# A four-layer graph network on one core: row statistics made in the stages ahead, and a fourth ScalarE evaluation per group in the second nucleus step

## The chip, the cores and the metric

The kernel runs on one core of a Trainium2 chip. The metric is the device time of one execution in microseconds (us), as the median over several runs. The core has five engines that work side by side and meet at semaphores: TensorE (PE in the profile, its weight loads PEld), VectorE (DVE), ScalarE (ACT), GpSimd (POOL) and SyncE (SP), which here only issues DMAs.

## The reference, cut to what matters

x is 2048 x 256, adj is 2048 x 2048. Each of four layers takes the row-normalised x, cuts it at zero and adds its result to x.

```python
h = relu(_layernorm(x)); x = x + L0(h)     # 8-head attention with adj as bias and mask
h = relu(_layernorm(x)); x = x + L1(h)     # two diffusion steps, then a layernorm with gamma and beta
h = relu(_layernorm(x)); x = x + L2(h)     # normalised adj @ h @ W.T + b
h = relu(_layernorm(x)); x = x + L3(h)     # relu(normalised (adj + I) @ h @ weight)

# L1, for each of two steps s:
Xf = Rf @ Xf;  Xb = Rb @ Xb
Xa = A @ Xa            # A = _adj_from_feats(Xa): softmax of the logits over the "nucleus" of each row
Z  = Z + (Xf @ U1[s] + Xb @ U2[s] + Xa @ U3[s])
# at the end: Y = X + Z, then (Y - mean) / sqrt(var + eps) * gamma + beta
```

The nucleus of a row holds its largest softmax weights until their sum reaches 0.9; the rest of the row is dropped and the row is normalised again.

## The kernel before, in words

The 2048 rows are held as T = 16 row blocks of 128 partitions. The program is a sequence of stages, each a block with one instruction stream per engine, with a barrier between blocks: setup, adjacency, `attend` (L0), then for step 0 and step 1 of L1 a `refresh` (called qk0 and qk1, which makes the logit factors) and a `nucleus` (nuc0 and nuc1), then `onward` (the end of L1 and the start of L2) and `last` (L2 and L3). Nothing plans the order at run time: on each engine it is the order in which the Python functions issue the instructions, and the semaphore waits between them decide the rest.

**attend.** For each of 8 heads and 16 row blocks TensorE makes logits (`qk`, L638), VectorE adds the bias and finds the row maximum (`peaks`, L786), ScalarE takes exp and rounds to fp16 (L706, L711), VectorE makes the fp16 remainder (`lo`, L800), SP turns both halves by DMA, and TensorE multiplies (`av`, L649). `add` (L811) adds to acc and `shift` (L870), in the last head, stores x with beta added to x_scratch. GpSimd makes two powers and one `partition_all_reduce` (L699) near the start and is then idle.

**refresh, with norm (qk0).** VectorE takes `bn_stats` and `bn_aggr` of acc in quads of four row blocks and adds eps; GpSimd takes the power -1/2 (L1370); VectorE makes the bias (`centre`, L1499); ScalarE writes the normalised rows (L1437); TensorE transposes them (L1386), and multiplies. TensorE also waits for `halved`, the halving of w3 (L1504) after its load.

**nucleus.** Rows are worked on in four groups of G = 4 row blocks. For each row block i = G*g + k TensorE makes the logits (L1687), VectorE finds the peak (L2024), ScalarE takes exp into e (L1882, `exp(g, k)`). Then a threshold per row is searched by C = 7 evaluations (step 1): an evaluation sums the weights of a row over a threshold, and `update` narrows the bounds. It is done in one of two ways:

- `cut(g, n)` on VectorE: four `mass` instructions (L2027), one per row block, and `update`.
- `sums(g, n)` on ScalarE: two instructions per row block, Relu and Sign with accumulation (L1896), which write their full output into PT (`aside`), and on VectorE `update_from_sums(g, n)`. VectorE asks for it with `aim(g)`; `next_sums(g, n)` is `update_from_sums` and `aim`. The constant BY_SUMS = 3 says how many of the seven are of this kind in groups 1 to 3 of step 1.

After the seven, `look(g)` settles the threshold, and `keep(g, n)` removes what is under it, with the ties, tile by tile (L2202, L2212). Each finished tile is multiplied: TensorE turns it (`multiply(g, k)`, L1702), ScalarE copies it in eight pieces into the two fp16 tiles PT (`halves(g, k)`, L1904 and L1906), and TensorE multiplies with the rows of x (L1720). The logits of group g + 1 share one PSUM buffer, so `logits(g + 1, k + 1)` waits for `exp(g + 1, k)`.

Beside that runs the diffusion of Xf and Xb (`diffuse`, L1620 to L1665) with ScalarE's part in `results`: `rows_of` (L1849), `turned_rows` (L1858, L1860) and `weighted_rows` (L1864, which writes y). In step 1 the row blocks 0 to 4 are diffused beside group 0 and 1, 5 to 8 after `multiply(0, 3)`, 9 to 12 after `multiply(1, 3)`, 13 to 15 after `multiply(2, 3)` (DIFFUSED = (5, 9, 13)). After each of the last three stands a row of `after(n)` (L1754 to L1760, L1917, L1919), which adds the last product of row block n to y. ScalarE's order in step 1, around the change:

```python
sums(1, 2)
for k in range(G):
    halves(0, k)
    exp(2, k)
    product(0, k)
for n in range(BY_SUMS):
    sums(2, n)
    results(range(DIFFUSED[0] + n, DIFFUSED[0] + n + 1), n > 0)
```

The last group is turned by `last_halves` (L1933) and `last_rests` (L2305, VectorE).

**onward.** For each quad of row blocks: statistics of y, a power on GpSimd (L985), y centred and multiplied by gamma (`centre`, L1077), added onto x (`onto`, L1085), statistics of x, a power, the bias (`aim`, L1092), the normalised rows on ScalarE (`normal`, L1030), transposes and the product with W on TensorE (L998, L1007), two cuts on ScalarE (L1045, L1048) and the remainder on VectorE (L1098). SP loads w2, W3, the row b, then x in four pieces, and when all have landed the 16 pieces of adjT, which `last` reads.

## Time and profile before

| what | value |
|---|---|
| median of 3 runs | 3354.73 us (3354.25 to 3355.26) |
| profiled execution | 3354.33 us, its span 3352.5 us |
| busy share of the span | PE 88%, PEld 66%, DVE 65%, ACT 40%, POOL 2% |
| mean granted TensorE clock | 0.953 |

The stages in the span: attend about 190 to 1890 us, qk0 to 1939, nuc0 to 2396, qk1 to 2412, nuc1 to 3100, onward to 3159, last to the end. The times below are microseconds from the start of the span. A row of a timeline gives the start, the duration, the engine, the line of the kernel, the operation and its operands, how many instructions are merged in it, and in brackets how long the engine had been idle before it and what released it. The line of an instruction is the one in the printed kernel. Buffer numbers are left out of names: nuc_e is e, nuc_l the PSUM banks, nuc_pThi and nuc_pTlo are PT, nuc_minus_t the negated threshold.

### The profile page before, as it was taken

The numbers are of one execution on the slowest core, as the hardware profiler recorded it, in microseconds if no ns is written. First come the engines' busy times: TensorE is split into PE (matmuls) and PEld (weight loads), VectorE is DVE, ScalarE is ACT, GpSimd is POOL, SyncE is SP. The second block draws the span as 40 slices with busy tenths as digits, with TensorE's granted clock in tenths as the row PEclk, the third lists the DMA queues.
The fourth block names the chain that finished last, engine by engine and source line by source line (L and its number), as shares of the span: only waits on it lengthen the run. The fifth ranks groups of instructions, "written<-read, shape, count | busy, mean of one in ns | idle before, by whom it ended". The sixth has DMA issues, their size and how long they took to land. (4 is left out here: it accounts for less than half of the span.)

```text
span 3352.5 us, 56595 instructions
## 1 busy us (share of the span) xinstructions
PE 2954.3 (88%) x20632; PEld 2221.0 (66%) x20632; DVE 2162.5 (65%) x4428; ACT 1349.0 (40%) x1750; POOL 57.8 (2%) x71
## 2 busy tenths in 40 slices
PE   3989999999999999999999778878884678687699
PEld 3966776767767677676776447656563556575588
DVE  7865655556555565555656488888588887885531
ACT  5844434444344443444434322333326355522321
POOL 0000000000000000000000000000000000000100
PEclk8999999999999999999999889999997889899899
DMA  7938748477484774847748412100010010100500
GB/s 265 410 133 200 183 119 199 114 190 186 118 199 114 189 186 118 200 114 190 185 119 213 100 57 89 39 5 23 26 39 26 1 51 11 41 26 1 232 1 26
DMA packets 587858, 396.82 MB, mean 118 GB/s; under 512 B 538563, under 2 KB 553414, under 8 KB 562118
## 3 DMA queue, kind: packets, MB, share of 16 engines
q1 hardware_dynamic: 585990, 382.49, 42.3%
q10 hardware_dynamic: 1728, 12.58, 1.1%
q8 instruction: 73, 1.20, 0.1%
q14 instruction: 67, 0.55, 0.0%
HBM read 223.05 MB, written 37.75 MB: 78 GB/s over the span
## 5 line engine op out<-in xcount | busy, mean ns | idle before, releaser
L800 DVE SCALAR_TENSOR_TENSOR e_lo<-e,e_hi 128x2048 f16<-128x2048 f32 x128 | 293.3, 2292 | 432.2 <-ACT e_hi L711 432.2
L649 PE MATMUL av<-vw_hi,pT_hi 128*128 128x256 f16 x2048 | 559.7, 273 | 6.2 <-DMA pT_lo<-e_lo 6.2
L649 PE MATMUL av<-vw_lo,pT_hi 128*128 128x256 f16 x2048 | 559.7, 273 | 0.0
L649 PE MATMUL av<-vw_hi,pT_lo 128*128 128x256 f16 x2048 | 559.7, 273 | 0.0
L638 PE MATMUL logits<-kT_hi,qT_hi 128*128 128x512 f16 x1024 | 389.6, 380 | 4.6 <-DVE att_small L786 4.0
L638 PE MATMUL logits<-kT_lo,qT_hi 128*128 128x512 f16 x1024 | 389.1, 380 | 0.0
L638 PE MATMUL logits<-kT_hi,qT_lo 128*128 128x512 f16 x1024 | 389.1, 380 | 0.0
L705 ACT ACTIVATE att_small<-att_small,minus 128x1 f32<-128x1 f32 x128 | 38.0, 297 | 772.9 <-DVE att_small L795 772.9
L786 DVE CUSTOM_DVE_ANT_0 e<-logits,bias,att_small 128x1024 f32<-128x1024 f32 x256 | 328.6, 1283 | 0.0
L2027 DVE SCALAR_TENSOR_TENSOR nuc_junk<-nuc_e,nuc_thr 128x2048 bf16<-128x2048 f32 x140 | 323.7, 2348 | 3.9
L706 ACT ACTIVATE e<-e,att_small,sc 128x2048 f32<-128x2048 f32 x128 | 266.5, 2082 | 0.0
L711 ACT ACTIVATE e_hi<-e 128x2048 f16<-128x2048 f32 x128 | 244.7, 1912 | 15.3
L649 PEld LDWEIGHTS av<-vw_hi,pT_hi 128*128 128x128 f16 x2048 | 200.9, 98 | 43.2 <-issue 6.7
L649 PEld LDWEIGHTS av<-vw_lo,pT_hi 128*128 128x128 f16 x2048 | 200.9, 98 | 36.3
L649 PEld LDWEIGHTS av<-vw_hi,pT_lo 128*128 128x128 f16 x2048 | 200.9, 98 | 23.8
L1687 PE MATMUL nuc_l<-logit_k,logit_q 128*128 128x512 f32 x256 | 133.9, 674 | 65.9 <-ACT nuc_e L1882 58.9
L638 PEld LDWEIGHTS logits<-kT_hi,qT_hi 128*128 (+1 forms) x1024 | 100.3, 98 | 123.1 <-issue 15.4
L638 PEld LDWEIGHTS logits<-kT_hi,qT_lo 128*128 (+1 forms) x1024 | 100.4, 98 | 121.6 <-issue 1.3
L638 PEld LDWEIGHTS logits<-kT_lo,qT_hi 128*128 (+1 forms) x1024 | 100.5, 98 | 107.2 <-issue 1.1
L1663 PE MATMUL nuc_l<-nuc_u,nuc_xsT 128*128 128x256 f32 x320 | 92.0, 444 | 77.2 <-ACT nuc_xsT L1860 68.6
L382 PE MATMUL adj_tp<-ident_one,adj_rows 128*128 128x129 f32 x512 | 123.1, 404 | 30.5 <-DVE adj_count L418 30.5
L382 PEld LDWEIGHTS adj_tp<-ident_one,adj_rows 128*128 128x128 f32 x512 | 123.0, 337 | 30.8 <-DVE adj_count L418 30.8
(427 smaller groups left out, 5777.0 us busy)
## 6 DMA issues: line engine op xcount, KB each, us to landing
bias<-bias_scratch SPq DMA_DIRECT2D x130, 1024.0 KB, 4.9
bias_scratch<-adj_bias SPq DMA_DIRECT2D x16, 1024.0 KB, 8.3
adjT_scratch<-adjT SPq DMA_DIRECT2D x16, 1024.0 KB, 8.5
nuc_at_hi<-adjT_scratch SPq DMA_DIRECT2D x32, 512.0 KB, 3.8
nuc_at_lo<-adjT_scratch SPq DMA_DIRECT2D x32, 512.0 KB, 4.6
adjT<-adjT_scratch SPq DMA_DIRECT2D x16, 1024.0 KB, 19.9
adj_rows<-in_adj_dram ACTq DMA_DIRECT2D x12, 1024.0 KB, 8.7
adj_rows<-in_adj_dram SPq DMA_DIRECT2D x4, 1024.0 KB, 14.0
```

Source lines behind the costliest of these rows:

```text
L382: last = nc.tensor.matmul(o, rows_u[:, t // 2, t % 2 * P:(t % 2 + 1) * P], ident1[:, :], start=True, stop=True)
L638: last = nc.tensor.matmul(o, QT[w][:, k, ds(t * P, P)], KT[x][:, k, c0:c0 + BANK], start=(k == 0 and w == x == 0), stop=(k == 1 and w == 1))
L649: last = nc.tensor.matmul(AV[par], PT[par][w][:, m, :], VW[x][:, m, :], start=(m == 0 and w == x == 0), stop=(m == T - 1 and w == 1))
L705: nc.scalar.activation(masked(par), nb(par), ACT.Exp, bias=minus[:, 0:1], scale=1.0)
L706: nc.scalar.activation(E[par][:, :], E[par][:, :], ACT.Exp, bias=nb(par), scale=sc[:, 0:1], accum_out=ssum(par)).then_inc(exped, 1)
L711: nc.scalar.activation(EH[:, :], E[par][:, :], ACT.Copy, scale=P_SCALE).then_inc(hi_s, 1)
L786: return nc.vector.tensor_tensor_reduce(E[par][:, cols], L[half][:, :], B[par][:, cols], 1.0, (small[:, par, 6:7], m0(par))[half], ALU.add ...
L800: nc.vector.scalar_tensor_tensor(out=EL[:, :], in0=E[par][:, :], scalar=P_SCALE, in1=EH[:, :], op0=ALU.mult, op1=ALU.subtract).then_inc(lo ...
L1663: nc.tensor.matmul(WEIGHTED, xT[:, n * D + k * P:n * D + (k + 1) * P], U[:, n, k, :], start=(n == k == 0), stop=False)
L1687: last = nc.tensor.matmul(scores_in(i)[:, b * BANK:(b + 1) * BANK], QT[:, i * P:(i + 1) * P], KT[:, b * BANK:(b + 1) * BANK], start=True, ...
L2027: nc.vector.scalar_tensor_tensor(out=void[:, k % 2, :], in0=e[:, g % 2, k, 0:N], scalar=bound[:, k:k + 1], in1=e[:, g % 2, k, 0:N], op0=co ...
```

## The change

1. **Sums.** BY_SUMS becomes 4 for step 1. In groups 1 to 3 evaluation 3 goes from VectorE (`cut(g, 3)`) to ScalarE (`sums(g, 3)`). It is asked for by `next_sums(g, 2)`, which `keep` of the group before now issues ahead of its fourth tile (`behind`), and read by `update_from_sums(g, 3)`. For groups 1 and 2 that stands behind the first peak of the next group. In ScalarE's program sums(1, 3) stands right behind sums(1, 2) and ahead of halves(0, 0); sums(2, 3) and sums(3, 3) stand ahead of the results of row blocks 8 and 12.
2. **Statistics of x for L1.** `attend` makes them in the last head, tile by tile, into `row_stats` (in the place of deg); qk0 only adds eps, takes the powers and makes the bias. A fourth power in attend's GpSimd program follows the all-reduce.
3. **Statistics of y.** At the end of nuc1, VectorE makes them for row blocks 0 to 11 and centres these; GpSimd takes their power. `onward` does it for the last quad only. Its order on VectorE is shorter, and SP loads the first piece of x ahead of w2 and b, and W3 last.
4. **Order.** In attend, ahead of the loop, peaks(1, 1) goes before lo(0, 0). The last head's items are written out instead of looped.

```diff
-        BY_SUMS = (1, 3)[step]
+        BY_SUMS = (1, 4)[step]
...
                 if step:
                     sums(1, 2)
+                    sums(1, 3)
...
                 for n in range((9, 4)[step]):
                     spread(n + 1)
+                if step:
+                    pl.wait_ge(tail_asked, 1)
+                    nc.gpsimd.tensor_tensor(y_rstd[:, 0:DONE], y_rstd[:, 0:DONE], halfp[:, 0:DONE], ALU.pow).then_inc(tail_powed, 1)
...
-                def keep(g, n):
+                def keep(g, n, behind={}):
...
                     for k in range(G):
+                        if k in behind:
+                            behind[k]()
                         load(G + k)
                         first_of_ties(g, k).then_inc(masked_s, 1)
...
-                    keep(0, 1)
-                    update_from_sums(1, 2)
+                    keep(0, 1, {3: lambda: next_sums(1, 2)})
                     peak(2, 0)
-                    cut(1, 3)
+                    update_from_sums(1, 3)
                     peak(2, 1)
...
-                    keep(1, 2)
-                    update_from_sums(2, 2)
+                    keep(1, 2, {3: lambda: next_sums(2, 2)})
                     peak(3, 0)
-                    cut(2, 3)
+                    update_from_sums(2, 3)
...
-                    keep(2, 3)
-                    update_from_sums(3, 2)
-                    for n in range(3, C):
+                    keep(2, 3, {3: lambda: next_sums(3, 2)})
+                    update_from_sums(3, 3)
+                    for n in range(4, C):
                         cut(3, n)
...
                 for k in range(G):
                     last_rests(k)
+                if step:
+                    v.wait_ge(c_done, DONE)
+                    for t in range(DONE):
+                        nc.vector.bn_stats(y_stats[:, t, :], y[:, t, :]).then_inc(tail_s, 1)
+                    v.wait_ge(tail_s, DONE)
+                    for t in range(DONE):
+                        nc.vector.bn_aggr(row_stats[:, t, :], y_stats[:, t, :]).then_inc(tail_s, 1)
+                    v.wait_ge(tail_s, 2 * DONE)
+                    nc.vector.tensor_scalar(y_rstd[:, 0:DONE], row_stats[:, 0:DONE, 1], LN_EPS, None, ALU.add).then_inc(tail_asked, 1)
+                    for t in range(DONE):
+                        nc.vector.scalar_tensor_tensor(out=y[:, t, :], in0=y[:, t, :], scalar=row_stats[:, t, 0:1], in1=gb[:, 0, :],
+                                                       op0=ALU.subtract, op1=ALU.mult).then_inc(tail_s, 1)
+                    v.wait_ge(tail_s, 3 * DONE)
```

In attend:

```diff
                 pl.wait_ge(ratios, 1)
                 nc.gpsimd.partition_all_reduce(top[:, 4:7], top[:, 0:3], P, ABSMAX).then_inc(largest, 1)
+                pl.wait_ge(largest, 1)
+                nc.gpsimd.tensor_tensor(top[:, 7:8], scales[:, 2, 0:1], halfp[:, 0:1], ALU.pow).then_inc(largest, 1)
...
+                def statistics(t):
+                    v.wait_ge(av_free, T * (HEADS - 1) + t + 1 + AV_FREE)
+                    nc.vector.bn_stats(summary, acc[:, t, :]).then_inc(summed_up, 1)
+                    v.wait_ge(summed_up, 2 * t + 1)
+                    nc.vector.bn_aggr(row_stats[:, t, :], summary).then_inc(summed_up, 1)
+                    v.wait_ge(summed_up, 2 * t + 2)
...
                 evacuate(0, 3)
+                link.wait()
+                peaks(1, 1, 1, link)
                 lo(0, 0, link)
-                peaks(1, 1, 1, link)
```

In refresh and onward:

```diff
-                    stats_of(0)
-                    v.wait_ge(w_loaded, 16 * 5)
-                    nc.vector.tensor_scalar(w3[:, :, :, :], w3[:, :, :, :], 0.5, None, ALU.mult).then_inc(halved, 1)
-                    for b in range(1, QUADS):
-                        stats_of(b)
-                        centre(b - 1)
+                    for b in range(QUADS):
+                        q = slice(QUAD * b, QUAD * (b + 1))
+                        nc.vector.tensor_scalar(rstd[:, q], mv[:, q, 1], LN_EPS, None, ALU.add).then_inc(stats_done, 1)
+                    for b in range(QUADS - 1):
+                        centre(b)
+                        if b == 1:
+                            v.wait_ge(w_loaded, 16 * 5)
+                            nc.vector.tensor_scalar(w3[:, :, :, :], w3[:, :, :, :], 0.5, None, ALU.mult).then_inc(halved, 1)
                     centre(QUADS - 1)
...
-                stats_of(0, 0)
-                stats_of(0, 1)
-                centre(0)
+                stats_of(0, 3)
                 row_scales()
                 onto(0)
                 stats_of(1, 0)
                 weights_in()
-                stats_of(0, 2)
+                onto(1)
                 aim(0)
-                centre(1)
-                onto(1)
                 stats_of(1, 1)
-                stats_of(0, 3)
+                centre(3)
+                onto(2)
                 aim(1)
-                centre(2)
-                onto(2)
                 stats_of(1, 2)
-                centre(3)
+                remainder(0)
                 aim(2)
-                remainder(0)
                 onto(3)
                 stats_of(1, 3)
                 remainder(1)
```

## Rows read from the trace of the kernel before

**Rows 1.** Windows: length; busy PE, PEld, DVE, ACT, POOL; PEclk, DMA share, GB/s

```profile
2412.00:3100.00 688.00, 507.10 (x3440) 399.87 (x3440) 547.08 (x1164) 293.04 (x416) 2.30 (x8) 0.89 0.08 27
2758.00:2776.00 18.00, 13.06 (x56) 9.19 (x57) 8.75 (x29) 4.41 (x12) 0.00 (x0) 1.00 0.02 8
```

**Rows 2.** Timeline of ACT, groups 1 to 2 (start us, us; released by)

```profile
2571.50 2.00 ACT L1896 ACTIVATE nuc_pThi<-nuc_e,nuc_minus_t 128x2048 f16<-128x2048 f32 x1 [5.84 <-DVEq L2019]
...
2590.24 0.60 ACT L1904 ACTIVATE nuc_pThi<-nuc_l 128x512 f16<-128x512 f32 x1 [2.73 <-PE nuc_l L1702]
...
2599.05 0.60 ACT L1906 ACTIVATE nuc_pTlo<-nuc_l 128x512 f16<-128x512 f32 x1 [0.48 <-PE nuc_l L1713]
...
2640.03 1.96 ACT L1882 ACTIVATE nuc_e<-nuc_l,nuc_nmax 128x2048 f32<-128x2048 f32 x1
...
2670.29 1.96 ACT L1882 ACTIVATE nuc_e<-nuc_l,nuc_nmax 128x2048 f32<-128x2048 f32 x1
```

**Rows 3.** Timeline of DVE, groups 1 to 2

```profile
2535.68 0.17 DVE L2061 SCALAR_TENSOR_TENSOR nuc_signs<-nuc_signs,nuc_half_t 128x4 f32<-128x4 f32 x1 [0.33 <-ACT nuc_pTlo L1896]
...
2538.95 2.35 DVE L2145 SCALAR_TENSOR_TENSOR nuc_junk<-nuc_e,nuc_hi 128x2048 f32<-128x2048 f32 x1
...
2607.99 0.09 DVE L2202 MATCH_VALUE_LOAD nuc_junk<-nuc_listed,nuc_e 128x8 f32 x1 [0.21 <-issue]
...
2620.02 2.29 DVE L2024 TENSOR_REDUCE nuc_nmax<-nuc_l 128x1 f32<-128x2048 f32 x1
...
2672.38 0.17 DVE L2040 TENSOR_SCALAR nuc_work<-nuc_Z 128x4 f32<-128x4 f32 x1 [3.40 <-ACT nuc_e L1882]
```

**Rows 4.** Timeline of ACT, groups 2 to 3

```profile
2736.67 0.60 ACT L1858 ACTIVATE nuc_xsT<-nuc_l 128x512 f32<-128x512 f32 x1
...
2743.20 0.39 ACT L1864 ACTIVATE y<-nuc_l 128x256 f32<-128x256 f32 x1 [4.92 <-PE nuc_l L1665]
...
2757.79 0.39 ACT L1864 ACTIVATE y<-nuc_l 128x256 f32<-128x256 f32 x1 [2.18 <-PE nuc_l L1665]
```

**Rows 5.** Timeline of DVE, groups 2 to 3

```profile
2756.55 0.09 DVE L2202 MATCH_VALUE_LOAD nuc_junk<-nuc_listed,nuc_e 128x8 f32 x1 [0.22 <-issue]
...
2778.24 2.29 DVE L2024 TENSOR_REDUCE nuc_nmax<-nuc_l 128x1 f32<-128x2048 f32 x1 [9.61 <-PE nuc_l L1687]
```

**Rows 6.** Timeline of ACT, group 3 and the tail

```profile
2921.36 0.39 ACT L1864 ACTIVATE y<-nuc_l 128x256 f32<-128x256 f32 x1 [2.18 <-PE nuc_l L1665]
...
2939.57 0.60 ACT L1904 ACTIVATE nuc_pThi<-nuc_l 128x512 f16<-128x512 f32 x1 [0.82 <-PE nuc_l L1702]
...
3045.45 2.07 ACT L1933 ACTIVATE nuc_pThi<-nuc_l 128x512 f16<-128x512 f32 x4
```

**Rows 7.** Timeline of DVE, group 3 and the tail

```profile
2920.18 0.09 DVE L2202 MATCH_VALUE_LOAD nuc_junk<-nuc_listed,nuc_e 128x8 f32 x1 [0.22 <-issue]
...
3059.12 2.47 DVE L2305 SCALAR_TENSOR_TENSOR nuc_pTlo<-nuc_l,nuc_pThi 128x512 f16<-128x512 f32 x4
```

**Rows 8.** Costliest groups, second nucleus step, shapes apart

```profile
L2027 DVE SCALAR_TENSOR_TENSOR nuc_junk<-nuc_e,nuc_thr 128x2048 bf16<-128x2048 f32 x76 | 175.7, 2348 | 2.2
```

**Rows 9.** Timeline of PE, start of attention and of qk0

```profile
251.96 0.60 PE L638 MATMUL logits<-kT_hi,qT_hi 128*128 128x512 f16 x1 [3.97 <-DVE att_small L786]
...
1903.98 0.87 PE L1386 MATMUL qk_tp<-ident,y 128*128 128x128 f32 x3 [14.74 <-ACT y L1437]
```

**Rows 10.** Timeline of POOL, first power of qk0

```profile
1900.46 2.05 POOL L1370 TENSOR_TENSOR qk_rstd<-qk_rstd,halfp 128x4 f32<-128x4 f32 x2 [1670.75 <-DVE qk_rstd L1494]
```

**Rows 11.** Timeline of DVE, qk0 and onward

```profile
1897.49 0.29 DVE L1504 TENSOR_SCALAR w<-w 128x256 f32<-128x256 f32 x1 [2.30 <-DMA w<-in_L_gnn_W_dram]
...
3102.46 1.40 DVE L1067 BATCH_NORM_STATS2 onw_stats<-y 128x6 f32<-128x256 f32 x4
...
3104.39 1.67 DVE L1077 SCALAR_TENSOR_TENSOR y<-y,onw_mv,gamma_beta 128x256 f32<-128x256 f32 x4
...
3115.86 0.15 DVE L1092 SCALAR_TENSOR_TENSOR onw_minus<-onw_mv,onw_rstd 128x4 f32<-128x4 f32 x1
```

More of the change, by code:

```diff
@@ L884, in _, with item, last_items, items @@
                 LINKS = 6
-                def items(h, ends=False):
+                def item(h, t, par, link):
+                    i = T * h + t
+                    lo(i + 1, 1 - par, link)
+                    peaks(i + 2, t + 2, par, link)
+                    add(i, t, par, link)
+                    masks(t + 3, 1 - par, link)
+                def last_items():
+                    link = Chain(v, chain, 10 + (HEADS - 1) * (LINKS * T))
+                    for t in range(T - 2):
+                        item(HEADS - 1, t, t % 2, link)
+                        shift(T * (HEADS - 1) + t, t, t % 2)
+                        statistics(t)
+                    return link
+                def items(h):
                     with v.Fori(0, T // 2 - 1) as j:
@@ L1350, in refresh @@
         with block:
-            if norm:
+            if norm is not None:
                 @block.sync
@@ L1433, in _ @@
                 for b in range(QUADS + 2):
-                    if norm and b < QUADS:
+                    if norm is not None and b < QUADS:
                         s.wait_ge(centred, b + 1)
@@ L1482, in cut @@
                             link.note(nc.vector.tensor_scalar(parts[1][:, t, :], rest[:, t, :], lo_gain, None, ALU.mult))
[L1484 to L1494 removed]
+                if norm is not None:
                     def centre(b):
@@ L1519, in _, with nucleus @@
                         nc.vector.tensor_copy(QT[:, b * BANK:(b + 1) * BANK], TP[b // 2][b % 2][:, :]).then_inc(w2_read, 1)
-def nucleus(nc, sb, ps, sem, name, QT, KT, parts, out, ident, diffusion, next_logits):
+def nucleus(nc, sb, ps, sem, name, QT, KT, parts, out, ident, diffusion, next_logits, tail):
     weights, at_d, scales, ident16, y, sc, Xp, Xf, Xb, step = diffusion
@@ L1541, in nucleus @@
     w2x, w3x = w2[:, :, :].rearrange("p a n -> p (a n)"), w3[:, :, :, :].rearrange("p k a n -> p k (a n)")
+    (tail_s, tail_asked, tail_powed) = (sem(f"{name}_tail_{s}") for s in ("stats", "asked", "powed"))
+    gb, halfp, row_stats, y_rstd = tail
+    DONE = T - G
     C = CUTS[step]
```

91 lines of the change are left out of this document (43 added, 48 removed).

## The prediction, made before the changed kernel was timed

> **What bounds the kernel now.** I read the windows by stage first, then for each place that the diff touches the timeline of each engine, and looked in it for the wait that ends last. The stage that changes most is the second nucleus step, 2412 to 3100 us, where VectorE is busy 547.08 of 688 us, TensorE 507.10 and ScalarE only 293.04 [rows 1]. The reader is to see that the half-idle ScalarE is no spare engine here: its rows stand in the order in which its program is written, and TensorE waits for it tile by tile.
>
> Between group 1 and group 2 ScalarE's row of sums(1, 2) starts at 2571.50; eight such rows of 2.0 us make 16.0. After them it copies the turned halves of tile 0, from 2590.24 to 2599.65, and then waits until VectorE has found peak(2, 0), which starts at 2620.02 and takes 2.29 [rows 2, 3]. From there the tiles follow each other by a loop through ScalarE and TensorE: exp(2, 1) at 2640.03 and exp(2, 3) at 2670.29, which is 15.13 us a tile, with no wait for VectorE ahead of either. It is VectorE that waits 3.40 us at 2672.38 for the last exp, before it can begin group 2 [rows 3]. So the loop and VectorE are about level, and the loop is slightly the longer.
>
> Between groups 2 and 3 it is plainer: VectorE waits 9.61 us for the logits of peak(3, 0), until 2778.24 [rows 5]. What it waits for is a queue of small steps that all begin after sums(2, 2): turned rows 2736.67, y 2743.20, y again 2757.79, then the last row block, four after(n) and the logits [rows 4]. Here ScalarE and TensorE already set the end.
>
> **The sums: what the edit takes away.** One evaluation a group is four rows of 2.35 us on VectorE [rows 8], 9.4 us, three times. Its update stays.
>
> **What it adds, group 1 to 2.** sums(1, 3) is asked for by the next_sums that now stands ahead of the fourth tile of keep(0, 1). That tile's first instruction stood at 2607.99; a next_sums costs 2538.95 - 2535.68 = 3.3 us [rows 3]; so ScalarE starts at 2611.3 and ends at 2627.3. In ScalarE's program these sums stand ahead of halves(0, 0), which before ran at 2590 under keep, at no cost. Now they run behind: 9.4 us to 2636.7, then exp(2, 0), which before started at 2622.3 behind the peak. Three times 15.13 later exp(2, 3) starts at 2682.1 against 2670.29: **11.8 us later**. I take the steady 15.13 for all three, since TensorE has just worked on halves(0, 0); the first interval of before, 2622.3 to 2640.03, was 17.7 us, which would make it 14.4. The 9.4 us that VectorE no longer works turn into waits: for sums(1, 3), for the logits ahead of each peak, and ahead of begin(2).
>
> **Group 2 to 3.** The fourth tile of keep(1, 2) stood at 2756.55 [rows 5]. Sums(2, 3) then runs from 2759.85 to 2775.85, both in the frame of before. ScalarE may not turn rows(7) ahead of it, as it did at 2749 under keep; that comes now after 2775.85. What follows is known piece by piece: turned rows, weighing at a TensorE that has just idled, y: 2736.67 to 2743.59, 6.9 us; then from the end of the y at 2757.79 (2758.18) through the last row block, four after(n) and logits(3, 0) to 2778.24, 20.1 us [rows 4, 5]. Between them before lay the matmuls of tile 8, which this time TensorE does while ScalarE sums. 2775.85 + 6.9 + 20.1 = 2802.8 against 2778.24: **24.6 us later**. The loop behind it was free of VectorE before and is unchanged.
>
> **Group 3.** Fourth tile of keep(2, 3) at 2920.18 [rows 7], sums(3, 3) to 2939.5, then 6.9 for y and 17.8 (2921.75 to 2939.57) to halves(2, 0): 2964.2 against 2939.57 [rows 6]. From there to last_halves(0) nothing of VectorE's is waited for, so last_halves(0) comes 24.6 later than 3045.45, at 3070.1. Before, 13 us of cover lay there: last_rests(0) started only at 3059.12, when VectorE had finished keep(3, 4) [rows 7]. VectorE gains little: from the start of the fourth tile it had 12.0 us for the tile and update_from_sums (2607.99 to 2620.02 [rows 3]) and 9.4 + 2.4 for an evaluation with its update, 23.8 to the end of cut(3, 3); now 3.3 + 16.0 + 3.1 = 22.4, since it waits for the sums. So the tail starts at 3070.1 + 0.6 instead of 3059.12: **11.6 us later**.
>
> Together 11.8 + 24.6 + 11.6 = +48.0 us.
>
> **The statistics.** At the front of attention peaks(1, 1) now goes ahead of lo(0, 0) on VectorE. TensorE waited 3.97 us for those reads at 251.96 [rows 9] and ran the next matmuls slowly after it. They can start with no wait, but then av(0) waits for the turned lo half, which leaves VectorE 1.9 us later; I take -2.5 us, bounds 0 and -4.0. The added bn_stats and bn_aggr per tile of the last head (about 0.7 us) lie in VectorE's waits for ScalarE and cost nothing; the last one lies under the store of x. If that cover were gone, 0.7.
>
> In qk0 the whole of TensorE waits 14.74 us, until 1903.98 [rows 9]. GpSimd's first power there starts at 1900.46 [rows 10], 5.3 us after it was asked for, although GpSimd had been idle since the all-reduce, 1670.75 us before; the edit puts a power behind that all-reduce, early in attention, and drops the statistics. Then ready comes near 1896.7 and the next condition is late: w3 halved at 1897.49 + 0.29 [rows 11]. Gain 1903.98 - 1897.9 = 6.1; bounds 2.3 (if the late start stays, only the statistics go) and 6.1. I take -6.0: the later powers of that stage start at once after their request.
>
> At the end of step 1 the statistics and centrings of twelve row blocks, three quads at 1.9 us (3102.46 to 3104.39) and 1.67 [rows 11], 10.7 us, follow last_rests(3) and end about 2 us ahead of TensorE's after(15). The power behind them pays the late start (5.3) and 1 to 3 us, and so ends about 1 us beyond the stage: +1.
>
> In onward the first aim stood at 3115.86, 15.3 us after the stage began. Ahead of it now: one quad of y statistics 1.9, the row scales about 1, two additions at 1.7 (as the centring), one quad of x statistics 1.9, the weights about 1, some 1.5 for x to land, since its load is now first on SP's queue ahead of both weights: 10.7 us. The chain behind it (ScalarE, TensorE, ScalarE) keeps its length, with aim(2) 0.6 us late behind remainder(0). Gain 4.5 less 0.5: -4, bounds -1 and -6. The adjT loads start behind the x loads as before and have some 6 us of slack at the end, of which 4 are used.
>
> **Sum.** 48.0 - 2.5 - 6.0 + 1.0 - 4.0 = +36.5. The profiled execution took 3354.33 (span 3352.5), 0.4 below the median of 3354.73, so the sum gives 3390.8 and 3391.2; I write 3391. From no change this kernel's runs can tell about 0.2%, 7 us.
>
> **Rivals.** (1) VectorE keeps setting the end, and ScalarE's queue is harmless. Then groups 1 and 2, where a peak of 2.3 hides more of the wait, save 23.8 + 2.3 - 22.4 = 3.7 each and group 3 1.4, the statistics 11.5: 3354.7 - 20.3 = 3334, faster. VectorE's high busy share speaks for it; the waits of 3.40 and 9.61 us against [rows 3, 5]. It decides if halves(0, 0) or turned rows(7) could run before the added sums, that is if exp(2, 0) could still start by about 2622. Chance 0.06.
> (2) Only the tail differs: the 13 us of cover turn out to hold all of group 3's delay, for example since results 13 to 15 close up. -11.6: 3379. Chance 0.08.
> (3) TensorE's clock stays at its low level, 1.2 GHz, through the thin chains. In 2758 to 2776 TensorE was busy 13.06 us at a granted clock of 1.00 (2.4 GHz), right after dense matmuls [rows 1]. After the added sums it comes from 20 us of idleness into the same thin work; at the low level these 13 us would double, in groups 2 and 3: +26, 3417. Chance 0.08. The Trainium skill, TensorE: Matmul & The Clock Gate, section A second HAM failure mode: psum-queue depth-cycling, says that an array with small idle gaps between its groups of matmuls can swing between the two levels; by that rule the time would go there, and the row at 1.00 in the same thin work speaks against it.
> (4) The fourth evaluation by sums is rounder than the exact one and some tile needs a retry, a bisection with a look: three to five rows of 2.35 us and small ones, 15 to 30 us a tile, 3406 to 3421. Against it: the 76 evaluations of before are just those of the plan, 7 x 4 for group 0 and 3 x 4 x 4 for the others [rows 8]; none is a retry's. Chance 0.03.
> My own case: 0.75.
>
> **Range.** My case alone 3380 to 3402 (the cold first interval +2.6, statistics +7 and -5, group 2 and 3 chains each 2 either way). 3377 to 3404 takes in (2) and leaves out (1), (3) and (4). Faster 0.06, same 0.02, slower 0.92.
>
> **What would show it.** In the second nucleus step the evaluation rows fall from 76 to 64. exp(2, 0) starts 9 to 10 us after the end of sums(1, 3); VectorE's wait at peak(3, 0) grows from 9.6 to over 25 us; last_rests(0) waits for ScalarE's copy; the stage is 734 to 738 us long. In qk0 the first power follows its request at once and TensorE starts near 1897 less 2.5. I am wrong if VectorE has no long wait at peak(3, 0), or if TensorE's granted clock in the chain of after(n) is near 0.5.

## The result and the profile after

The changed kernel took 3391.71 us in the median of four runs (3385.20 to 3396.22), the kernel before 3354.6 on the same chip (3354.25 to 3355.26). The ratio is 1.0111, 95% interval 1.0099 to 1.0123: slower by 37.1 us, where 36.5 was predicted. The profiled execution is the longest of the four: 3396.22 us, span 3394.3, which is 41.8 over the span of before. The times of the rows below are compared with those of before in this one execution; it stands 4.5 us over the median, and the paragraph on the clock looks at that.

The windows of the second nucleus step (the two edges of [rows 1], each moved as the stage's own events moved) and of the chain of four after(n) ahead of group 3 (columns as in [rows 1]):

```profile
2403.12:3141.80 738.68, 512.29 (x3440) 402.78 (x3440) 531.12 (x1189) 340.37 (x464) 4.78 (x9) 0.86 0.08 25
2788.00:2806.00 18.00, 12.81 (x56) 9.09 (x56) 0.00 (x0) 4.60 (x12) 0.00 (x0) 1.00 0.00 1
```

The stage has grown from 688 to 738.7 us. VectorE does 16 us less in it and ScalarE 47 us more, TensorE has the same number of matmuls (3440). The evaluation rows on VectorE (costliest groups of this stage, shapes apart) have fallen from the 76 of [rows 8] to 64:

```profile
L2051 DVE SCALAR_TENSOR_TENSOR nuc_junk<-nuc_e,nuc_thr 128x2048 bf16<-128x2048 f32 x64 | 148.0, 2348 | 1.9
```

ScalarE's timeline through the three places (start us, us; in brackets the idle time ahead and what ended it):

```profile
2602.65 2.00 ACT L1916 ACTIVATE nuc_pThi<-nuc_e,nuc_minus_t 128x2048 f16<-128x2048 f32 x1 [22.72 <-DVEq L2043]
...
2618.67 0.60 ACT L1924 ACTIVATE nuc_pThi<-nuc_l 128x512 f16<-128x512 f32 x1
...
2629.24 1.96 ACT L1902 ACTIVATE nuc_e<-nuc_l,nuc_nmax 128x2048 f32<-128x2048 f32 x1
...
2644.38 1.96 ACT L1902 ACTIVATE nuc_e<-nuc_l,nuc_nmax 128x2048 f32<-128x2048 f32 x1
...
2674.65 1.96 ACT L1902 ACTIVATE nuc_e<-nuc_l,nuc_nmax 128x2048 f32<-128x2048 f32 x1
...
2765.12 2.00 ACT L1916 ACTIVATE nuc_pThi<-nuc_e,nuc_minus_t 128x2048 f16<-128x2048 f32 x1 [17.01 <-DVEq L2043]
...
2781.14 0.60 ACT L1878 ACTIVATE nuc_xsT<-nuc_l 128x512 f32<-128x512 f32 x1
...
2788.13 0.38 ACT L1884 ACTIVATE y<-nuc_l 128x256 f32<-128x256 f32 x1 [5.39 <-PE nuc_l L1685]
...
2793.80 0.38 ACT L1884 ACTIVATE y<-nuc_l 128x256 f32<-128x256 f32 x1 [3.38 <-PE nuc_l L1685]
...
2809.02 0.60 ACT L1924 ACTIVATE nuc_pThi<-nuc_l 128x512 f16<-128x512 f32 x1 [3.49 <-PE nuc_l L1722]
...
2953.11 2.00 ACT L1916 ACTIVATE nuc_pThi<-nuc_e,nuc_minus_t 128x2048 f16<-128x2048 f32 x1 [16.80 <-DVEq L2043]
...
2994.21 0.60 ACT L1924 ACTIVATE nuc_pThi<-nuc_l 128x512 f16<-128x512 f32 x1 [0.82 <-PE nuc_l L1722]
...
3101.76 2.06 ACT L1953 ACTIVATE nuc_pThi<-nuc_l 128x512 f16<-128x512 f32 x4
```

The first row is the start of sums(1, 3). It was asked for at the fourth tile of keep(0, 1), and ScalarE had stood idle 22.72 us until then, with the turned halves of tile 0 waiting behind it in its program: in the kernel before [rows 2] they were copied at 2590.24. Now they come at 2618.67, and exp(2, 0) 10.6 us after the sums' end. From exp(2, 1) to exp(2, 3) it is 15.13 us a tile, exactly as before. The same picture stands at sums(2, 3) (17.01 us idle, then y at 2788.13, y at 2793.80, halves(1, 0) at 2809.02) and at sums(3, 3) (16.80 idle, halves(2, 0) at 2994.21).

VectorE's timeline of the same places, and of the start of onward:

```profile
2618.67 0.16 DVE L2085 SCALAR_TENSOR_TENSOR nuc_signs<-nuc_signs,nuc_half_t 128x4 f32<-128x4 f32 x1 [4.59 <-ACT nuc_pTlo L1916]
...
2635.09 2.29 DVE L2048 TENSOR_REDUCE nuc_nmax<-nuc_l 128x1 f32<-128x2048 f32 x1 [13.22 <-PE nuc_l L1707]
...
2676.74 0.17 DVE L2064 TENSOR_SCALAR nuc_work<-nuc_Z 128x4 f32<-128x4 f32 x1 [4.55 <-ACT nuc_e L1902]
...
2808.58 2.29 DVE L2048 TENSOR_REDUCE nuc_nmax<-nuc_l 128x1 f32<-128x2048 f32 x1 [34.16 <-PE nuc_l L1707]
...
3102.39 2.48 DVE L2331 SCALAR_TENSOR_TENSOR nuc_pTlo<-nuc_l,nuc_pThi 128x512 f16<-128x512 f32 x4 [15.97 <-ACT nuc_pThi L1953]
...
3146.99 1.67 DVE L1115 SCALAR_TENSOR_TENSOR acc<-y,y_rstd,acc 128x256 f32<-128x256 f32 x4 [1.66 <-DMA acc<-x_scratch]
...
3155.03 0.69 DVE L1133 COPY l_wT<-l_tp 128x512 f32<-128x512 f32 x1 [4.32 <-PE l_bc L1046]
...
3157.67 0.16 DVE L1122 SCALAR_TENSOR_TENSOR onw_minus<-onw_mv,onw_rstd 128x4 f32<-128x4 f32 x1
```

The work taken from VectorE has turned into waits: 4.59 us for the sums, 13.22 ahead of peak(2, 1), 34.16 ahead of peak(3, 0) where [rows 5] has 9.61, and 15.97 at last_rests(0), which now waits for ScalarE's copy; in [rows 7] it had no wait.

TensorE at the start of attention, at the start of qk0 and in onward:

```profile
256.24 0.27 PE L652 MATMUL av<-vw_hi,pT_hi 128*128 128x256 f16 x1 [2.63 <-DMA pT_lo<-e_lo]
...
1894.38 1.97 PE L1410 MATMUL qk_tp<-ident,y 128*128 128x128 f32 x8 [8.59 <-DVE w L1522]
...
3152.74 1.11 PE L1045 MATMUL l_tp<-ident,l_w 128*128 128x128 f32 x4 [11.84 <-DMA l_w<-in_L_gnn_weight_dram]
```

GpSimd's powers:

```profile
237.32 0.59 POOL L704 TENSOR_TENSOR tops<-scales,halfp 128x1 f32<-128x1 f32 x1 [7.18 <-issue]
1890.00 3.95 POOL L1394 TENSOR_TENSOR qk_rstd<-qk_rstd,halfp 128x4 f32<-128x4 f32 x4 [1652.09 <-DVE qk_rstd L1517]
...
3133.80 2.48 POOL L2030 TENSOR_TENSOR y_rstd<-y_rstd,halfp 128x12 f32<-128x12 f32 x1 [92.38 <-DVE y_rstd L2486]
```

In qk0 the four powers now start at 1890.00 without a pause, and TensorE starts at 1894.38 instead of 1903.98 [rows 9]; its last condition is the halved w3.

| part | predicted | profile after against before |
|---|---|---|
| attention | -2.5 | -3.4 (last av ends 1885.79, before 1889.24) |
| qk0 | -6.0 | -6.2 (TensorE -9.6 in all) |
| step 0 and qk1 | 0 | +0.7 (first exp of step 1 at 2412.57, before 2421.45) |
| group 1 to 2 | +11.8 | +13.2 (exp(2, 3) 4.36 later, the step's first exp 8.88 earlier) |
| group 2 to 3 | +24.6 | +26.0 (peak(3, 0) 30.34 later, less 4.36) |
| group 3, tail | +11.6 | +11.5 (onward 41.8 later, less 30.3) |
| tail power | +1.0 | 0 |
| onward | -4.0 | 0 (59.2 us long, as before) |
| sum | +36.5 | +41.8 |

### The profile page after: what moved, and what is told of

It reads as the page before. It is cut to its first block and busy times, and to the rows that moved or that the text cites. A ratio compares the mean times of both kernels' runs of the same rounds, so it can differ in the third digit from the quotient of the medians.

```text
span 3394.3 us, 56556 instructions
## 1 busy us (share of the span) xinstructions
PE 2960.8 (87%) x20632; PEld 2225.4 (66%) x20632; DVE 2136.7 (63%) x4414; ACT 1394.4 (41%) x1798; POOL 57.2 (2%) x70
## 5 line engine op out<-in xcount | busy, mean ns | idle before, releaser
L2051 DVE SCALAR_TENSOR_TENSOR nuc_junk<-nuc_e,nuc_thr 128x2048 bf16<-128x2048 f32 x128 | 295.9, 2348 | 3.6
L641 PEld LDWEIGHTS logits<-kT_hi,qT_hi 128*128 (+1 forms) x1024 | 100.0, 98 | 119.2 <-issue 11.2
L1683 PEld LDWEIGHTS nuc_l<-nuc_u,nuc_xsT 128*128 128x128 f32 x320 | 71.1, 231 | 139.8 <-ACT nuc_xsT L1880 115.7
## 6 DMA issues: line engine op xcount, KB each, us to landing
adj_rows<-in_adj_dram SPq DMA_DIRECT2D x4, 1024.0 KB, 13.7
```

The costliest lines, as they stand in the source:

```text
L641: last = nc.tensor.matmul(o, QT[w][:, k, ds(t * P, P)], KT[x][:, k, c0:c0 + BANK], start=(k == 0 and w == x == 0), stop=(k == 1 and w == 1))
L1683: nc.tensor.matmul(WEIGHTED, xT[:, n * D + k * P:n * D + (k + 1) * P], U[:, n, k, :], start=(n == k == 0), stop=False)
L2051: nc.vector.scalar_tensor_tensor(out=void[:, k % 2, :], in0=e[:, g % 2, k, 0:N], scalar=bound[:, k:k + 1], in1=e[:, g % 2, k, 0:N], op0=co ...
```

## The experiments

The kernel before was run again beside them, and each ratio is to those of its runs that are named below. Medians in us:

| kernel | median | runs | ratio, 95% interval |
|---|---|---|---|
| stats_only | 3339.32 | 3336.53 to 3342.12 | 0.9957, 0.9944 to 0.9971 |
| sums_only | 3405.11 | 3403.22 to 3407.25 | 1.0152, 1.0138 to 1.0166 |
| order12 | 3371.58 | 3367.03 to 3379.10 | 1.0053, 1.0039 to 1.0066 |
| onward_late | 3341.32 | 3332.94 to 3343.44 | 0.9956, 0.9942 to 0.9970 |
| early_ask | 3341.79 | 3337.37 to 3348.35 | 0.9965, 0.9951 to 0.9978 |
| early_g3 | 3333.51 | 3330.07 to 3344.43 | 0.9939, 0.9926 to 0.9953 |
| sums_g3 | 3363.02 | 3356.60 to 3364.74 | 1.0028, 1.0017 to 1.0039 |
| no_power | 3345.35 | 3341.63 to 3351.05 | 0.9978, 0.9969 to 0.9987 |
| peaks_first | 3350.66 | 3343.94 to 3355.88 | 0.9993, 0.9984 to 1.0002 |
| best | 3332.27 | 3328.12 to 3335.45 | 0.9932, 0.9918 to 0.9945 |

The kernel before had 3354.20 (beside the first four), 3353.59 (the next four) and 3352.19 (the last two), over 9, 17 and 15 runs; these spread from 3345.6 to 3357.3. Kernels from different ones of these three groups can be compared less closely than the intervals say, since the median of before itself moved by up to 2.4 between them and the first result.

**The two halves of the change (stats_only, sums_only).** The edit of stats_only, on the changed kernel:

```diff
-        BY_SUMS = (1, 4)[step]
+        BY_SUMS = (1, 3)[step]
-                    sums(1, 3)
-                    keep(0, 1, {3: lambda: next_sums(1, 2)})
+                    keep(0, 1)
+                    update_from_sums(1, 2)
-                    update_from_sums(1, 3)
+                    cut(1, 3)
```

and the same in groups 2 and 3. sums_only is the reverse of it, on the kernel before.

> The changed kernel with three ScalarE evaluations a group again, everything else of the edit kept. My theory: the fourth sums are all of the loss and the statistics and reordering keep their gain, which the changed kernel's trace shows as 3.4 us in attention and 6.2 in qk0 and none later: 3354.7 - 9.6 = 3345, and the whole step from here to the changed kernel is 46 to 50 us. Rival, that the parts hide each other (VectorE's shorter tail in the second nucleus step only comes to bear together with fewer VectorE evaluations): 3335 or 3354. The long waits of VectorE at peak(2, 0) and peak(3, 0) are then those of before: none and 9.6 us.

> The kernel before with the fourth ScalarE evaluation in groups 1 to 3 and nothing else. My theory: +48.0 us by the prediction's three terms (11.8, 24.6, 11.6), by the changed kernel's trace +49.4, so 3403 to 3405. Rival (the statistics in the tail are part of the loss): under 3395. If the spread of 11 us between runs of the changed kernel comes from the sums, it is seen here and not in the kernel with the statistics alone.

Measured: -14.9 and +50.9 us, together +36.0 against the 37.1 of the whole. So the parts add up and don't hide each other, and the rival that the tail's statistics are part of the loss falls. The size of the statistics' gain was missed, though: 3339.3 lies as near to the 3335 of the rival as to my 3345, and the step from here to the changed kernel is 52.4 instead of 46 to 50. VectorE's wait at peak(3, 0) is 8.41 us, and at peak(2, 0) there is none, as in before. In the trace of sums_only exp(2, 3) comes 13.7 later than in before, peak(3, 0) 39.0 and the first row of onward 50.2, so the three terms are 13.7, 25.3 and 11.2 (each the difference to the one before). Of the 5 us between 9.6 and 14.9 the paragraph on the clock tells what is known; in the one trace of stats_only 7.0 of the 18.0 us by which onward starts earlier than in before lie between TensorE's start in qk0 and the first exp of step 1. The spread of 11 us is not shown to belong to the sums: both kernels spread by 4 to 6 us here.

**ScalarE's order (order12).** On the changed kernel:

```diff
-                    sums(1, 3)
                 for k in range(G):
                     halves(0, k)
+                    if step and k == 0:
+                        product(0, 0)
+                        sums(1, 3)
                     exp(2, k)
...
                 for n in AFTER[0]:
                     after(n)
+                if step:
+                    sums(2, 3)
                 for k in range(G):
                     halves(1, k)
```

> The changed kernel with another order of ScalarE's program in groups 1 and 2 alone: halves(0, 0) and the copy of its product ahead of sums(1, 3), and results(8), last_result(8) and the four after(n) ahead of sums(2, 3). My theory, that the loss is what stands behind the sums in ScalarE's order: exp(2, 0) comes 5 us after that of before instead of 12 (its own 0.3 us behind the sums' end), halves(1, 0) 11 to 12 after it instead of 26, group 3 unchanged at 11.5: 28 instead of 49, so 21 us faster than the changed kernel, near 3370. Rival, that ScalarE's order is harmless and the wait of VectorE for the sums is the loss: no change, 3390. A second rival, that VectorE becomes the bound behind group 2: 3375 to 3380.

Measured 3371.58, 20.1 less than the changed kernel, where 21 was expected. ScalarE's timeline:

```profile
2597.27 2.00 ACT L1916 ACTIVATE nuc_pThi<-nuc_e,nuc_minus_t 128x2048 f16<-128x2048 f32 x1 [7.80 <-DVEq L2048]
...
2613.29 1.97 ACT L1902 ACTIVATE nuc_e<-nuc_l,nuc_nmax 128x2048 f32<-128x2048 f32 x1
...
2764.73 1.99 ACT L1916 ACTIVATE nuc_pThi<-nuc_e,nuc_minus_t 128x2048 f16<-128x2048 f32 x1
...
2780.74 0.60 ACT L1924 ACTIVATE nuc_pThi<-nuc_l 128x512 f16<-128x512 f32 x1
...
2791.29 1.96 ACT L1902 ACTIVATE nuc_e<-nuc_l,nuc_nmax 128x2048 f32<-128x2048 f32 x1
```

exp(2, 0) stands right behind the sums, and sums(2, 3) follows the last after(n) without a pause. Counted from the step's first exp, exp(2, 3) is 4.3 later than in before (expected 5), halves(1, 0) 12.1 beyond that (expected 11 to 12), peak(3, 0) 4.0 and exp(3, 3) 18.0, the first row of onward 30.1 (expected 28). The rival that ScalarE's order is harmless falls. VectorE as the next bound isn't seen either: it waits 13.18 us at peak(3, 1).

**When the sums are asked for (early_ask, early_g3, sums_g3).** One argument of the changed kernel differs in early_ask, in each of the three groups:

```diff
-                    keep(0, 1, {3: lambda: next_sums(1, 2)})
+                    keep(0, 1, {1: lambda: next_sums(1, 2)})
```

> The changed kernel with the fourth sums asked for ahead of the second tile of keep instead of the fourth, in all three groups; four evaluations by sums a group and ScalarE's order as in the changed kernel. My theory, that the loss is only where the sums stand in time: group 1 sums(1, 3) ends 18 us earlier and halves(0, 0) is done ahead of peak(2, 0), so 0 to +0.5 against before instead of 12; group 2 6 to 7 later than before instead of 25; group 3: last_halves(0) 6 later and VectorE's keep 8.5 earlier, so the tail 7 earlier than before instead of 11 later. Together near 0 against before's stage, and with the statistics 3339 (3335 to 3344), 52 faster than the changed kernel. Rival, that the 48 us of more ScalarE work themselves lie on the path wherever they stand: 3380 to 3390.

Measured 3341.79: 49.9 less than the changed kernel, with all of the 48 us of sums that it had added to ScalarE (24 rows of 2.0) still there. ScalarE in group 1 to 2:

```profile
2583.33 2.00 ACT L1916 ACTIVATE nuc_pThi<-nuc_e,nuc_minus_t 128x2048 f16<-128x2048 f32 x1 [4.48 <-DVEq L2043]
...
2599.34 0.60 ACT L1924 ACTIVATE nuc_pThi<-nuc_l 128x512 f16<-128x512 f32 x1
...
2613.19 1.97 ACT L1902 ACTIVATE nuc_e<-nuc_l,nuc_nmax 128x2048 f32<-128x2048 f32 x1 [2.56 <-DVE nuc_nmax L2048]
```

and VectorE at peak(3, 0):

```profile
2776.91 2.29 DVE L2048 TENSOR_REDUCE nuc_nmax<-nuc_l 128x1 f32<-128x2048 f32 x1 [16.78 <-PE nuc_l L1707]
```

The turned halves of tile 0 are copied at 2599.34, ahead of the peak, and exp(2, 0) waits for VectorE again, 2.56 us. Against the step's first exp, exp(2, 3) is 0.1 later than in before (expected 0 to 0.5), peak(3, 0) 8.8 later (expected 6 to 7) and onward 1.4 later (expected near 0). The rival that the added work itself is the price falls.

> The statistics kernel (three sums in groups 1 and 2) with four in group 3 alone, the fourth asked for ahead of the second tile of keep(2, 3). My theory: in group 3 VectorE sets the tail (13 us of cover over ScalarE and TensorE), so taking 8.5 us from it and giving ScalarE and TensorE 6 starts the tail 7 us earlier: 3339.3 - 7.2 = 3332. Rival, that ScalarE and TensorE lose as much as VectorE gains: 3339.

Measured 3333.51, 5.8 less than stats_only, where 7.2 was expected; the two intervals still touch (0.9926 to 0.9953 and 0.9944 to 0.9971). The trace gives 3.4 us against stats_only, from exp(3, 3) to the first row of onward, and 4.0 against before. What came short of the working stands in ScalarE's rows and in VectorE's row of last_rests(0):

```profile
2897.73 0.38 ACT L1886 ACTIVATE y<-nuc_l 128x256 f32<-128x256 f32 x1 [5.09 <-PE nuc_l L1687]
2898.01 1.99 ACT L1918 ACTIVATE nuc_pThi<-nuc_e,nuc_minus_t 128x2048 f16<-128x2048 f32 x1
...
2914.03 0.60 ACT L1880 ACTIVATE nuc_xsT<-nuc_l 128x512 f32<-128x512 f32 x1
```

```profile
3047.79 2.48 DVE L2332 SCALAR_TENSOR_TENSOR nuc_pTlo<-nuc_l,nuc_pThi 128x512 f16<-128x512 f32 x4 [4.10 <-ACT nuc_pThi L1955]
```

The fourth sums did not start when they were asked for: y of row block 10 stood ahead of them in ScalarE's program and came at 2897.73. Moved so that exp(3, 3) stands where it stands in before, the sums start at 2906.9 instead of 2904.7, and last_rests(0) waits 4.10 us for the copy: behind an early enough ask ScalarE, not VectorE, sets the tail.

> The kernel before with the fourth sums in group 3 alone, asked for as in the changed kernel, ahead of the fourth tile. By the prediction's term: +11.6, 3366, with halves(2, 0) 24.6 later, last_halves(0) 24.6 later and last_rests(0) 11.6 later. Rival, that groups 1 and 2 set up group 3's loss: less than 5. The second rival of the prediction (the 13 us of cover hold it): 3354.

Measured 3363.02, 9.4 us over before, in place of 11.6. ScalarE's halves(2, 0) and VectorE's last_rests(0):

```profile
2955.68 0.60 ACT L1906 ACTIVATE nuc_pThi<-nuc_l 128x512 f16<-128x512 f32 x1 [0.82 <-PE nuc_l L1704]
```

```profile
3062.28 2.48 DVE L2309 SCALAR_TENSOR_TENSOR nuc_pTlo<-nuc_l,nuc_pThi 128x512 f16<-128x512 f32 x4 [12.68 <-ACT nuc_pThi L1935]
```

The profile of this kernel runs 7.4 us ahead of that of before at exp(3, 3). Against that, halves(2, 0) is 23.6 later, last_rests(0) 10.6 and onward 9.1. So most of the 13 us of cover held and the rest came through, as the prediction has it; that the cover holds all of it falls, and so does the rival that groups 1 and 2 prepare the loss.

**The late power (no_power).** stats_only without the two lines that put a power behind the all-reduce.

> The statistics kernel without the power behind the all-reduce early in attention. In the kernel before, the first power after an all-reduce starts 7.2 us after GpSimd reaches it in its program (7.18 behind the all-reduce in the changed kernel; in qk0 of before about 7 us behind the start of the stage, although its input was there 5.3 us before). My theory: the first power of qk0 starts 6 to 7 us later than in the statistics kernel, near 1895.5, TensorE's first transpose of qk0 6 us later, 3345. Rival, that the statistics made earlier are the whole gain in qk0: no change, 3339.

Measured 3345.35, 6.0 us over stats_only. GpSimd in qk0,

```profile
1897.00 4.00 POOL L1392 TENSOR_TENSOR qk_rstd<-qk_rstd,halfp 128x4 f32<-128x4 f32 x4 [1666.82 <-issue]
```

and VectorE's first rows of the stage, which ask for them:

```profile
1889.65 0.38 DVE L1515 TENSOR_SCALAR qk_rstd<-deg 128x4 f32<-128x4 f32 x4 [2.33 <-PEq L127]
```

The request stands at the very start of the stage, and the powers come 7.35 us behind it. In before the stage's first VectorE row starts at 1893.17, the request follows 2 us later, behind the statistics, and the power at 1900.46 [rows 10]: 7.29 us behind the stage's start too. The lateness counts from there and not from the request, so the earlier request alone gives nothing at the power. TensorE's first transpose starts 7.2 us later than in stats_only (1900.50 and 1893.31), 1.0 of it from attention. So the gain in qk0 is that one power behind the all-reduce: without it TensorE waits 14.82 us at the start of qk0, with the statistics made earlier, and 14.74 in before, with none.

What the late power waits for can be seen in the rows of GpSimd's sequencer, in the view of one line (durations in ns, then first and last start in us). First the line of qk0's powers in before, then in no_power, then in the changed kernel the power directly behind the all-reduce and that of the tail:

```profile
L1370 POOLq MODIFY_POOL_CONFIG  x2: 11/11/11, 1893.2 to 1893.2; - x2
L1392 POOLq MODIFY_POOL_CONFIG  x2: 11/11/11, 1889.7 to 1889.7; - x2
L704 POOLq MODIFY_POOL_CONFIG  x2: 83/83/83, 230.1 to 230.1; - x2
L2030 POOLq MODIFY_POOL_CONFIG  x2: 11/11/11, 3041.4 to 3041.5; - x2
```

The powers themselves start at 1900.46, 1897.00, 237.32 and 3133.80: 7.2, 7.3 and 7.2 us after these rows in the first three, and in the tail as soon as their input is there. The line of qk0's powers in the changed kernel (L1394) has no such row, and its power follows the request at once. So the lateness belongs to this change of GpSimd's configuration, from the all-reduce to a power, and not to its idleness.

**The front of attention (peaks_first).** In the kernel before, `peaks(1, 1, 1, link)` goes ahead of `lo(0, 0, link)`.

> The kernel before with peaks(1, 1) ahead of lo(0, 0) at the front of attention, nothing else. The prediction put it at -2.5 us (bounds 0 and -4); the changed kernel's trace shows the first av 3.55 us earlier and the last one 3.4. My theory: -3.4, TensorE's 3.97 us wait ahead of the logits gone and 2.6 us of wait ahead of av(0), for the turned lo half, in its place, with TensorE at a granted clock of 1.00 in between instead of 0.80: 3350. Rival, that attention's end is set by VectorE or the DMAs, so that the start is made up for: 3353.6.

Measured 3350.66, 1.5 us less than before, an interval of the ratio that takes in 1. In the trace av(0) starts 3.3 us earlier (256.45 and 259.79), and the last av ends only 1.2 earlier (1888.02 and 1889.24), with a wait of 5.59 us for the transposed half ahead of it, 3.77 in before. So more than half of what is won at the front is lost on the way. In the changed kernel 3.4 us are left at the end. The other 2 us come with the rest of the edit in attention (the last head is written out there and has its statistics), which was not tried by itself, so their cause is not shown: in the eight traces with the whole edit in attention the last av ends at 1884.50 to 1886.37, in the three without any of it at 1889.05 to 1890.62.

**Onward (onward_late, best).** On stats_only:

```diff
                 stats_of(1, 0)
-                weights_in()
-                onto(1)
                 aim(0)
+                onto(1)
+                weights_in()
                 stats_of(1, 1)
                 centre(3)
-                onto(2)
                 aim(1)
+                onto(2)
```

> The statistics kernel (stats_only) with VectorE's order in onward changed: the first aim ahead of the copy of the transposed weights, the second aim ahead of the additions of quad 2. In the changed kernel VectorE waited 4.32 us ahead of that copy, for w2, which landed 10.4 us after the stage began, behind the first quad of x. My theory, that this wait ate the gain of the stage: aim(0) near 9.6 us after the stage's first row instead of 15.4, the stage 3.5 us shorter, 3341.5 against 3345. Rival, that the end of the stage is set by the 16 loads of adjT or by TensorE's chain: no change against stats_only.

Measured 3341.32, no change against 3339.32. The trace shows the stage shorter: from its first VectorE row to GpSimd's first in the last stage it is 55.8 us instead of 59.5, 3.7 less; but then TensorE enters the last stage slowly. Windows of the first 10 us of that stage, first onward_late, then stats_only (with its window of step 0, for the paragraph on the clock), then early_g3:

```profile
3144.00:3154.00 10.00, 9.88 (x64) 7.79 (x65) 1.44 (x4) 0.00 (x0) 5.50 (x8) 0.70 0.01 2
```

```profile
2260.00:2300.00 40.00, 31.18 (x180) 22.00 (x179) 35.62 (x65) 15.30 (x33) 4.42 (x2) 1.00 0.05 15
3142.00:3152.00 10.00, 10.00 (x92) 8.96 (x93) 1.58 (x4) 0.00 (x0) 5.48 (x8) 1.00 0.00 1
```

```profile
3147.00:3157.00 10.00, 10.00 (x66) 7.85 (x67) 1.57 (x4) 0.00 (x0) 5.47 (x8) 0.70 0.00 0
```

TensorE is busy nearly all the time in all three; the granted clock is 0.70, 1.00 and 0.70, and where it is 0.70 the last stage is 195.6 us long instead of 192.7: 2.9 us are lost. early_g3 has onward's order of stats_only, so the low clock does not come from the order of onward_late. In the trace neither the loads of adjT nor TensorE's chain kept the stage from getting shorter; that the shorter stage makes the kernel faster, the median of onward_late doesn't show. best is early_g3 with this order.

> The kernel with statistics and the early fourth sums in group 3 (early_g3), with VectorE's order in onward of onward_late as well. In onward_late the onward stage was 3.5 us shorter, and TensorE came into the last stage at a granted clock of 0.70 where the statistics kernel had 1.00, which gave 2.9 us of it back. My theory: the stage is 3.5 shorter again, and what is left of it depends on that clock: 3330 where it is 1.00, 3333 where it is near 0.70. Rival, that the low clock there was a chance of one execution: 3330 in the median.

Measured 3332.27, the fastest version here, 0.9932 of before. In its trace the stage is 3.2 us shorter than in early_g3 (56.1 and 59.3) and the first matmuls of the last stage run at a granted clock of 1.00, with the order of onward_late, which had 0.70. So neither order is tied to either clock, as the rival has it; the median is 1.2 less than early_g3's, within the spread, and a gain of 3 us in time is not shown.

**The clock.** The window from 2260 to 2300 us holds the end of step 0, which no edit touches: the same chain of small products as the after(n) of step 1. In stats_only (above) its granted clock is 1.00. In the changed kernel:

```profile
2260.00:2300.00 40.00, 32.77 (x167) 22.39 (x164) 35.16 (x67) 12.59 (x28) 4.42 (x2) 0.87 0.08 27
```

0.87 is a mixture of the two levels, 2.4 and 1.2 GHz. From TensorE's start in qk0 to the first exp of step 1, with the same code in between but for small rows at the start of qk0, it is 509.1, 509.2 and 510.5 us in the three traces with 1.00 in that window (sums_g3, peaks_first, stats_only), and 514.1 to 518.2 in the nine others, with 0.87 to 0.94, the changed kernel at 518.2 and before at 517.5 among them. Row by row, the changed kernel is 1.6 us behind stats_only at 2216, 3.5 at 2260, when the chain begins, and 7.4 at 2300. before and sums_g3 have the same instructions up to here: before is 0.3 us behind at 2280 and 6.4 at 2320. So several us of a single execution go with this chain's clock, which is of the size of the spread of the runs. Part of the 5 us that I can't place in the statistics' gain can be this; whether the median of stats_only has it is not shown, since each kernel has one trace. What makes the level in one execution and not in another wasn't found.

## Why the prediction was right

**ScalarE's queue as the price of the sums: right.** The three terms were 11.8, 24.6 and 11.6; sums_only gives 13.7, 25.3 and 11.2, and order12 and early_ask take 20 and 50 us of the loss away without taking a single sum away. Signs named ahead: evaluations 76 to 64, seen. exp(2, 0) 9 to 10 us after the sums: 10.6, a little outside. TensorE's start in qk0 near 1894.5, 1894.38. VectorE's wait at peak(3, 0) over 25, 34.16. last_rests(0) waits for ScalarE, 15.97. Stage 734 to 738 long, 738.7, a little over. Group 1 to 2 was undersized by 1.4 to 1.9. In the changed kernel the fourth sums start 0.2 us later than the working has them (190.08 after the step's first exp, 189.85 in the working), and the remaining 1.2 is the copy of tile 0's halves, from its first row to exp(2, 0): 10.57 us at a granted clock of 0.76, where the working took the 9.41 of before, at 0.90. In sums_only the two are 1.2 and 0.7 (10.10 us at 0.79). Why the sums start later there is not explained.

**Rivals.** That VectorE sets the end (3334) is false at the two inner places. At the tail it was true of the kernel before and no longer of the changed one (15.97 us of wait); early_g3 used the room there. That the cover holds the tail's delay is false by sums_g3. The low clock in the chain of after(n) did not come in step 1: 12.81 us busy at 1.00 in the window 2788 to 2806, against 13.06 in [rows 1]. It did come just ahead of it, behind the idleness that the added sums cause, and held for one product:

```profile
2782.07 5.49 PE L1683 MATMUL nuc_l<-nuc_u,nuc_xsT 128*128 128x256 f32 x12 [22.80 <-ACT nuc_xsT L1880]
...
2790.47 2.86 PE L1683 MATMUL nuc_l<-nuc_u,nuc_xsT 128*128 128x256 f32 x12 [0.96 <-ACT nuc_xsT L1880]
```

The same twelve matmuls take 5.49 us for one row block and then 2.86 for the next; in group 3 it is 5.48 and 2.86. So the low level costs 2.6 us at each of the two places and not 26 in all, and the sum had it already: its 6.9 us are those of such a product in before, 5.13 us behind 10.24 of idleness (2737.60). In step 0 the chain itself is partly at the low level in nine of the twelve traces, with the sums or without. So the mechanism was real, and its extent and its place were wrong. The rule of the Trainium skill that the prediction weighed (TensorE: Matmul & The Clock Gate, section A second HAM failure mode: psum-queue depth-cycling), that small idle gaps between groups of matmuls can make the array swing between its levels, agrees with the 0.87 of step 0 and not with the 1.00 of step 1. The 64 evaluations are 28 and three times 12: no retry.

**qk0: right in size and cause.** -6.0 predicted, -6.2 in the trace, 6.0 in no_power. The bound was w3's halving, as named. Wrong was the lower bound of 2.3 for the case that the late start stays: no_power has that case, and nothing is left of the gain (14.82 us of wait against 14.74).

**Attention: a term with the right sign.** -2.5 against -3.4 in the whole change and -1.5 for the edit alone, which is not clear of the noise.

**The tail's power, +1: the step that failed is "the power behind them pays the late start".** It started at 3133.80, as soon as it was asked for. GpSimd had reached it in its program 92 us earlier, and changed its configuration then (3041.4). The lateness counts from the moment when the engine reaches the instruction (no_power), so where the input comes later than that it is hidden. The working took it from the request, 5.3 us in [rows 10], and put it behind every long idleness. The kernel before had such a late power in onward as well, 7.7 us behind the change of configuration at 3100.5, for which VectorE waited 2.34 us; the working doesn't name it, and the edit moved it under the tail.

**Onward, -4: the step that failed is "the weights about 1".** The working moved w2's load behind the first quad of x on SP's queue and counted only x's side of it. w2 landed 10.4 us after the stage began (TensorE's 11.84 us wait; in before its transposes ran 3.6 us after the stage's start), VectorE waited 4.32 us for its transposes ahead of aim(0), and aim(0) came 15.35 us after the stage's first row, as in before 15.34. With this wait moved behind the first aim the stage is 3.7 shorter in the trace.

That the total came within 0.6 us was partly luck. By medians the sums cost 50.9 where 48.0 was predicted, and the rest of the edit gained 14.9 where 11.5 was: two misses of about 3 that cancel. In the traces the total was nearer than its parts too: of the profiled 41.8, the sums took 2.7 more than predicted, onward and the tail's power 3 more, attention and qk0 1.1 less, and step 0 and qk1 0.7; against the medians the profiled difference was 4.7 too large.

## What to carry to other kernels

Before work is moved to an engine that is half idle, ask what stands behind it in that engine's order and when it can be asked for: here the same 48 us of sums cost 50 us when asked for at the fourth tile, and when asked for at the second 1.4 in the trace and 2.5 between the medians (early_ask and stats_only). A load that is moved back on a queue has a reader of its own; follow the reader of both loads that change places. A gain that lies in a thin chain has to be judged over many runs, since in this kernel the stretch around one such chain differed by up to 9 us between executions of nearly the same code.

## What the runs showed of the hardware that was not expected

- The first power on GpSimd behind a `partition_all_reduce` starts about 7 us after the engine reaches it, whether or not its input is there: 7.18 us in the changed kernel, directly behind the all-reduce, and 6.90 to 7.10 in six others. If the engine waits at it for longer (92 us in the tail), none of this is seen. Later powers start at once. In the view of its line two sequencer rows MODIFY_POOL_CONFIG stand where the engine reaches it, and a power without them is not late. The Trainium skill, GPSIMD Engine Reference, section 2.1 Instruction dispatch, says that the first call of a freshly loaded kernel pays a load of code of about 6 us without an instruction in the profile; the 6.9 to 7.2 us here agree with it in kind and are a little longer (7.7 in onward of before).
- The same small products ran at a granted clock of 1.00 in some executions and 0.87 to 0.94 in others, with nothing changed ahead of them that the profile shows. Behind 22.80 us of idleness twelve matmuls took 5.49 us instead of 2.86, and the four after(n) that followed ran at 1.00 throughout.
- The last stage, dense matmuls in the same order in every kernel, began at a granted clock of 1.00 in eight of the twelve traces and was 192.7 us long; in four it began at 0.70 to 0.87 and was 194.0 to 195.6 long. In onward_late (0.70) and stats_only (1.00) TensorE had been busy 9.91 and 9.88 us in the 17 us ahead of it.
